# Keys' stage: ScalarE instead of VectorE normalises the rows of x

## The reference, cut to what matters

```python
xn = _layernorm(x, axis=-1)            # (x - m) / sqrt(v + 1e-5), for each row
x = x + gnn(xn, edge_index, ...) + linear_attention(xn[None], Wq, Wkv, Wproj, bproj)[0]
x = x + lstm_layer(_layernorm(x), ...)

# in linear_attention: keys are elu(k) + 1, and the context is a sum over all rows
k = jax.nn.elu(k) + 1.0
k_sum = k.sum(axis=2)
context = jnp.einsum('bhnd,bhne->bhde', k, v)
```

## Time and profile before

| | us |
|---|---|
| median of 3 runs | 2197.34 |
| lowest, highest | 2193.83, 2198.04 |
| the profiled execution | 2199.32 |
| its span | 2197.5 |
| DVE, ACT, PE busy in the span | 1598.0, 1186.0, 1941.3 |
| DVE, ACT, PE busy at 0 to 184 us | 146.48, 103.39, 125.95 |

### The profile page before, as it was taken

One profiled execution on the slowest core, in us unless ns is written; L12 is line 12 of the kernel. 1 busy time (PEld: TensorE's weight loads), 2 busy tenths in 40 slices (PEclk: granted clock), 3 DMA queues, 4 the chain that ended last, 5 costly groups with the idle time before them and its releaser, 6 DMA issues.

```text
span 2197.5 us, 42640 instructions
## 1 busy us (share of the span) xinstructions
PE 1941.3 (88%) x13254; PEld 1547.4 (70%) x13254; DVE 1598.0 (73%) x4208; ACT 1186.0 (54%) x3147; POOL 197.2 (9%) x274
## 2 busy tenths in 40 slices
PE   5679989999999999999989989996679998899845
PEld 4567876666666666666658878885468887888833
DVE  7887878777777777777737967777876666566687
ACT  4574445555555555555534446666875665566527
POOL 3352001000000000000002200000000000000060
PEclk8799998999999999999999999997569999899975
DMA  4222320100100100100115312223543343234403
GB/s 126 87 80 83 95 98 21 34 24 26 33 24 26 32 25 26 32 26 26 31 46 163 90 51 112 112 112 126 162 138 102 123 125 111 86 123 125 120 2 117
DMA packets 96796, 170.48 MB, mean 78 GB/s; under 512 B 8213, under 2 KB 68841, under 8 KB 96384
## 3 DMA queue, kind: packets, MB, share of 16 engines
q1 hardware_dynamic: 67693, 86.80, 12.2%
q10 hardware_dynamic: 27248, 77.11, 11.4%
q0 software_dynamic: 1744, 5.21, 0.8%
HBM read 110.53 MB, written 58.56 MB: 77 GB/s over the span
## 4 chain that ended last, share of the span: by engine, by line
PE 59%; DVE 21%; ACT 10%; issue 8%; POOL 2%; DMA 1%; DVEq 0%; ACTq 0%; POOLq 0%; SPq 0%
PE psum L665 28%; PE psum L814 11%; PE psum L660 7%; PE psum L771 4%; ACT scr L1121 2%; DVE scr L1503 2%; ACT scr L1129 2%; DVE scr L1713 2%; DVE bufB L1715 1%; DVE bufB L1630 1%; DVE scr L1711 1%; PE psum L848 1%; ACT scr L1088 1%; DVE bufA L1831 1%; PE psum L609 1%
## 5 line engine op out<-in xcount | busy, mean ns | idle before, releaser
L665 PE MATMUL psum<-halves,counts 128*128 128x512 f32 x2401 | 759.5, 423 | 16.3 <-ACT counts L1026 16.3
L1528 DVE TENSOR_TENSOR wx<-rs_buf 128x392 bf16<-128x392 bf16 (+1 forms) x1568 | 545.3, 391 | 211.4 <-PE psum L660 207.7
L1026 ACT ACTIVATE counts<-psum 128x392 fp32r<-128x392 f32 x784 | 391.4, 499 | 356.4 <-PE psum L660 355.0
L814 PE MATMUL psum<-bufB,wx 128*128 128x125 f32 x3392 | 425.3, 284 | 32.2 <-DVE bufB L1715 21.2
L814 PEld LDWEIGHTS psum<-bufB,wx 128*128 128x128 f32 x3392 | 401.3, 194 | 56.3 <-DVE bufB L1715 37.8
L665 PEld LDWEIGHTS psum<-halves,counts 128*128 128x128 f32 x2401 | 393.8, 190 | 65.9 <-ACT counts L1026 21.8
L660 PEld LDWEIGHTS psum<-wx 128*128 128x128 bf16 x3136 | 170.6, 99 | 198.5 <-issue 191.6
L660 PE MATMUL psum<-wx 128*128 128x98 bf16 x3136 | 284.7, 213 | 4.0 <-DVE wx L1528 2.9
L771 PE MATMUL psum<-bufA,wx 128*128 (+1 forms) x800 | 181.7, 379 | 3.2 <-POOL rs_buf L526 3.2
L771 PEld LDWEIGHTS psum<-bufA,wx 128*128 128x128 f32 x800 | 147.9, 190 | 20.7 <-issue 3.4
L1129 ACT ACTIVATE scr<-scr 128x125 f32<-128x125 f32 x280 | 86.4, 309 | 120.9 <-DVE scr L1713 115.6
(11 more groups left out here) (262 smaller groups left out, 2521.5 us busy)
## 6 DMA issues: line engine op xcount, KB each, us to landing
bufA<-gates_of_x ACTq DMA_DIRECT2D x136, 500.0 KB, 3.4
gates_of_x<-bufB SPq DMA_DIRECT2D x24, 1000.0 KB, 3.9
x_times_eps_plus_sums<-scr SPq DMA_DIRECT2D x50, 128.0 KB, 1.7
sums_by_feature<-scr SPq DMA_DIRECT2D x50, 128.0 KB, 1.9
scr<-x_times_eps_plus_sums SPq DMA_DIRECT2D x49, 128.0 KB, 2.1
wx<-in_x_dram SPq DMA_DIRECT2D x25, 250.0 KB
x_plus_mix<-wx SPq DMA_DIRECT2D x25, 250.0 KB, 4.8
bufB<-x_plus_mix SPq DMA_DIRECT2D x25, 250.0 KB, 2.7
```

What stands on the lines that cost most here:

```text
L665: return mm(psum[:, 3 + v, :], cnt[v][:, hi, :], xhl[:, hi, :, :].rearrange("p s d -> p (s d)"), start=(hi == 0), stop=(hi == NT - 1))
L814: return mm(gate_half(u, m, gate), whhv[:, k, (2 * gate + m) * P:(2 * gate + m + 1) * P], h, start=False, stop=(k == 1), skip_group_check= ...
L1026: fn(cnt[v][:, :, c * u:c * (u + 1)], psum[:, CB[u % 4], 0:PER * KEYS].rearrange("p (c h) -> p h c", h=NT), ACT.Copy).then_inc(S["c_sb"], 1)
L1528: last = tt(to, tab2[:, 0:k_, :].unsqueeze(1).broadcast_to([P, PER // 2, k_, 2]), keysT[v][:, part_, g0:g0 + PER // 2, :].unsqueeze(2).bro ...
```

## The change

ScalarE now normalises the rows: x * rstd + shift, as one activation (Identity) with a scale and a bias per row. VectorE computes the shift, -mean * rstd, for the whole chunk at once, behind the reciprocal (`row_scale`). ScalarE's new `row_norm` waits for it on its first tile of a chunk. The places in ScalarE's loop are the same as they were in VectorE's: after the scaled row of tile i-1, two tiles at i % 5 == 2, two at 3, one at 4. For the first chunk ScalarE does five normalisations right behind the square root, ahead of the copies L949. A buffer `shift` of 128x5 is added, twice.

```diff
@@ -175,6 +175,7 @@
         stats = sb("stats", XT * 6)
         mv = [sb(f"mv{v}", XT * 2) for v in range(2)]
         rstd = [sb(f"rstd{v}", XT) for v in range(2)]
+        shift = [sb(f"shift{v}", XT) for v in range(2)]
         eps_ln = sb("eps_ln", 1)
         tick = sb("tick", 32)
         ctxb = sb("ctxb", 2 * P)[:, :].rearrange("p (a n) -> p a n", a=2)
@@ -943,7 +944,16 @@
                 fn(rstd[q % 2][:, 0:h], mv[q % 2][:, :].rearrange("p (t c) -> p t c", c=2)[:, 0:h, 1], ACT.Sqrt,
                    bias=eps_ln[:, :]).then_inc(S["ln_std"], 1)
 
+            def row_norm(q, j):
+
+                if j == 0:
+                    act.wait_ge(S["ln_r"], 2 * q + 2)
+                fn(x_ring[q % XR][:, j, :], x_ring[q % XR][:, j, :], ACT.Identity, bias=shift[q % 2][:, j:j + 1],
+                   scale=rstd[q % 2][:, j:j + 1]).then_inc(S["xn_ok"], 1)
+
             row_std(0)
+            for j in range(XT):
+                row_norm(0, j)
             for n, (_, to) in enumerate(groups):
                 act.wait_ge(S["tr_ps"], n + 1)
                 fn(to, psum[:, 4 + n, :].rearrange("p (j n) -> p j n", j=4), ACT.Copy).then_inc(S["tr_sb"], 1)
@@ -983,6 +993,11 @@
                                       row_out[:, 2:j + 1, :]).then_inc(S["row_in2"], 16)
                 if i % XT == 1 and i // XT + 1 < XCH:
                     row_std(i // XT + 1)
+                q, j = i // XT + 1, i % XT
+                if j >= 2 and q < XCH:
+                    for j_ in ((0, 1), (2, 3), (4,))[j - 2]:
+                        if j_ < len(tiles(q)):
+                            row_norm(q, j_)
 
             act.wait_ge(S["lo_q"], NT)
             act.wait_ge(S["ld_small"], 128)
@@ -1287,14 +1302,14 @@
                         last = dve.bn_aggr(mv[q % 2][:, 2 * t:2 * t + 2], stats[:, 6 * t:6 * t + 6])
                     last.then_inc(S["ln_v"], 1)
 
-            def row_norm(q, j):
-
-                if j == 0:
-                    dve.wait_ge(S["ln_std"], q + 1)
-                    dve.reciprocal(rstd[q % 2][:, 0:len(tiles(q))], rstd[q % 2][:, 0:len(tiles(q))]).then_inc(S["ln_r"], 1)
-                    dve.wait_ge(S["ln_r"], q + 1)
-                ts(x_ring[q % XR][:, j, :], x_ring[q % XR][:, j, :], mv[q % 2][:, 2 * j:2 * j + 1],
-                   rstd[q % 2][:, j:j + 1], ALU.subtract, ALU.mult).then_inc(S["xn_ok"], 1)
+            def row_scale(q):
+
+                h = len(tiles(q))
+                dve.wait_ge(S["ln_std"], q + 1)
+                dve.reciprocal(rstd[q % 2][:, 0:h], rstd[q % 2][:, 0:h]).then_inc(S["ln_r"], 1)
+                dve.wait_ge(S["ln_r"], 2 * q + 1)
+                stt(shift[q % 2][:, 0:h], mv[q % 2][:, :].rearrange("p (t c) -> p t c", c=2)[:, 0:h, 0], -1.0,
+                    rstd[q % 2][:, 0:h], ALU.mult, ALU.mult).then_inc(S["ln_r"], 1)
 
             def row_cut(t):
 
@@ -1420,8 +1435,7 @@
 
             for j in range(XT):
                 row_stats(0, j)
-            for j in range(XT):
-                row_norm(0, j)
+            row_scale(0)
             dve.wait_ge(S["tr_sb"], 4)
             dve.memset(psum[:, 6, :], 0.0).then_inc(S["m_z"], 1)
             constants()
@@ -1445,10 +1459,8 @@
                         small_vectors()
                         for j_ in range(XT):
                             row_stats(1, j_)
-                    if j >= 2 and q < XCH:
-                        for j_ in ((0, 1), (2, 3), (4,))[j - 2]:
-                            if j_ < len(tiles(q)):
-                                row_norm(q, j_)
+                    if j == 2 and q < XCH:
+                        row_scale(q)
                     q, j = (t - 1) // XT + 2, (t - 1) % XT
                     if t and q < XCH and j < len(tiles(q)):
                         row_stats(q, j)
```

## The result

The change makes the kernel slower: 2206.66 us in the median of six runs (2202.66 to 2213.00), beside 2196.44 for the kernel before (2193.83 to 2198.32). The ratio is 1.0045, with an interval of 1.0034 to 1.0056: about +10 us, where 2196.0 was forecast and 2203.0 was the upper end of the range.

What follows compares the result with a forecast made beforehand. No engine was simply the bound: VectorE, ScalarE and TensorE form a ring in the keys' stage. Gains and losses by period sum to -1.35 us, on the median 2197.34 giving 2196.0 us; range 2190.5 to 2203.

Steps and rivals of the forecast that it cites:

- Added to VectorE: Ten shift instructions of 128x5 in the keys' stage, taken at 0.16 us each, bounds 0 and 0.21.
- A new wait: ScalarE's first normalisation of a period waits for VectorE's shift: start at 140.50, copy 1.61 us later, next minimum +1.10 us.
- T0: Reference time in a clean period: the minimum of the period's second tile, 139.12 us in the profile before.
- the second clean period: The period from 148.6 us, without other VectorE work on top: same steps, one mask wait of 0.21 less, -0.1 us.
- The tail: End of the keys' stage, from the minimum at 166.36: no statistics left to hide anything, +1.1 us.
- Opening: Before the first period: five normalisations delay ScalarE's weight copies 2 us, but VectorE stands 4.06 us for a DMA: 0.
- a ring that loses behind ScalarE's wait what VectorE wins: Keys' stage: at a period's first two normalisations the next minimum comes 1.10 us later, against 1.07 us VectorE had spent.
- ScalarE's normalisation: 49 Identity activations of 128x256 on ScalarE: 0.51 us each from start to start, bounds 0.40 and 0.60, 2.55 per period.
- Short masks: VectorE's masking after a late minimum takes 0.28 us, not 0.70, bringing the high part forward by 0.35 us.
- ScalarE becomes the bound: Rival: ScalarE's part grows 3.14 us a period, waits don't absorb it, TensorE's clock may stay low; +7.2, 2204.5 us; chance 0.13.
- The relief rival: VectorE was the bound and is relieved: 13.8 us won in six periods, less 1.4; 2184.9 us; chance 0.17.
- A wait for ln_r far from 0.6 us: Sign that the forecast is wrong: ScalarE's wait for VectorE's shift, put at 0.59 us a period, differs much.

Runs made afterwards that it cites:

- e8: Kernel before, with all five normalisations of a chunk moved on VectorE into its idle stretch ahead of the second tile's sum; 0.9948 times the kernel before.
- e9: Changed kernel with reciprocal and shift placed between VectorE's minimum and mask of the third tile, not behind the mask; 1.0005 times the kernel before.
- e11: The changed kernel timed again without any edit, on another chip; 1.0055 times the kernel before.
- e3: Changed kernel without the 49 normalisations, done by nobody; reciprocal and shift stay on VectorE; 0.9955 times the kernel before.
- e1: Changed kernel with reciprocal and shift moved ahead of the second tile's sum, where VectorE waits for the exponential; 1.0001 times the kernel before.
- e4: Kernel before plus 44 extra Identity activations on ScalarE into a spare buffer, waiting for nothing; VectorE normalises as before; 1.0011 times the kernel before.
- e12: Kernel before with all five normalisations in VectorE's idle stretch and 44 extra ScalarE activations into a spare buffer; 0.9994 times the kernel before.
- e2: Changed kernel with the shift's instruction issued twice, the first into a spare buffer; 1.0058 times the kernel before.

## Why the prediction was wrong

The failed step is "*Added to VectorE*", the shift at 0.16 us with bounds of 0 and 0.21, and with it "*A new wait*", by which ScalarE starts at 140.50. The shift takes 0.69 there, so ScalarE starts at T0 + 1.89 and not T0 + 1.38: 0.51 us later, and with everything queued behind it. It is a term of the right kind and the wrong size, and it explains about half of the miss. The bounds came from the reciprocal, the row of the same shape. The place should have given them. In the trace of before, GpSimd's low half starts ahead of the instruction behind the reciprocal, which starts at 140.29:

```profile
...
140.24 0.73 POOL L469 TENSOR_TENSOR halves<-wx,scr 128x256 fp32r<-128x256 f32 x1 [0.23 <-DVE scr L1306]
...
```

The pair of normalisations that stood there took 1.15, where e8's five take 1.70. The Trainium skill (VectorE: DVE Perf Modes, "Two Vector instructions with no wait between them") has a Vector instruction with two SBUF tensor inputs read the second through an interface shared with GpSimd. The shift, which reads `mv` and `rstd`, and the reciprocal, which reads one buffer, agree with it: 0.69 against 0.18 beside a running GpSimd instruction (the reciprocal's case is e9). Two inputs aren't all that matters in these rows, though: the mask has one, and takes 0.70 beside GpSimd's addition and 0.28 without it.

A check of its price in time: e11 and e9 differ by 8.5 us of earlier starts and by 10.8 us. On a straight line between them, an estimate that puts all of e9's gain down to the earlier starts, 0.51 us in nine stretches are worth 5.8 us, and at one for one 4.6, of the 11.6 between the forecast's -1.35 and +10.2.

How far it goes in single stretches: the second clean period ran at full clock throughout; forecast -0.1, and 0.51 more is +0.4; measured +0.46. The tail: 1.1 + 0.51 = 1.6; measured +1.75. Over nine stretches the term is 4.6 us, which would turn the forecast's -1.35 into +3.2. The stage end moved by 7.3 with the opening 1.07 earlier, so the nine stretches gave 8.4: 9.7 more than forecast, 4.6 of it by this term.

Some 2.7 us more stand in the first matmuls behind the late copies. At 29.6, 53.2, 128.9 and 145.4 us they took 2.08, 2.07, 2.07 and 1.52, against 1.69 and three times 1.13 before. They are longer because TensorE went wholly or partly at its lower clock; why it did there stays open. Nor was the clock lower throughout: from 22.6 us on the first stretch had 0.69 before and 0.76 after, that from 67.6 us 0.68 and 0.76. The remaining 2.4 us lie mainly in three stretches, by the table less these two terms: 0.9 in the one from 135.2, 0.7 in that from 22.6 and 0.4 in that from 42.8; no single row answers for them. This splitting of the last five us is read from the profiles, not tested, and the two us by which the medians moved more are not in it: here the profile of before, on which the forecast was built, is itself slow. Its wait of 4.06 us, against 1.9 to 3.2 in five kernels with the same opening, is what made "*Opening*" a 0.

Point by point:
- The mechanism, a ring that loses behind ScalarE's wait what VectorE wins, had the right parts. e3, e1 and the change stand at -10, 0 and +10: the relief, ScalarE's work, and the wait. Its balance was wrong: the first pair loses 1.96 us (the next minimum at T0 + 4.86 for + 2.90) and not 1.10, against 1.07 won. Of the 0.86 more, about 0.5 are the shift and 0.39 the matmul at 1.52.
- ScalarE's normalisation: 0.51 from start to start was right (143.95 to 144.95 for two is 0.50). The shift "done at 140.47" is 140.45 by its own terms, which changes nothing. No table load was added.
- Short masks came as forecast: 284 ns in the median after, 704 before. What they gave was less than the wait took.
- VectorE and ScalarE at 40 to 60 us: forecast near 18 and near 11, measured 16.99 and 11.11.
- The rival "*ScalarE becomes the bound*" had the right sign and named 2204.5, and its own sign came true: the clean stretch from T0 to the next table load, 9.49 before, is 11.65 after, over the 10.4. Its conditions hardly did: activations of 0.59 us, and at 40 to 60 us a clock of 0.83 against 0.84. ScalarE's work costs little while VectorE is late (e4), but 10 us once VectorE is relieved (e12), which is the change's case; that part of the rival was right, and the relief of e3 pays for it (e1). What turned the sum to a loss is a dear wait. "A wait for ln_r far from 0.6 us" was named as what would show the forecast wrong. Counted as there, from 0.46 us after the scaled row, it is 1.10.
- The relief rival: relief alone is worth 10 us (e3), near its 12.4, but ScalarE's share takes all of it back even without the dear wait (e1).

Whether the forecast's own wait of 0.59 us would have given 2196 isn't measured, and the runs speak against it. e9, with ScalarE 0.44 us earlier than in the forecast, stands at +0.5 (1.0005, 0.9996 to 1.0014), and the straight line from there to e11 passes the forecast's start at about +5.5. So about half of the miss lies outside the shift's term. The profiles point at the longer matmuls and the opening; no run tests it, and the cause of that half stays open.

## What to carry to other kernels

When work moves to another engine, price the small instruction that the new wait hangs on by its place, not by its shape: what GpSimd does at that moment, and what is queued in order behind the waiting engine. In a ring of engines moving work gives little either way (e1); first look for a stretch where the engine that has the work stands idle for another's table load, and put the work there (e8, -0.5%). A load that costs 2.4 us while another engine is late (e4) costs some 10 once that engine has been relieved (e12). And a difference of half a per cent should not be worked out on a single profile: this one held a wait of 4.06 us that was 1.9 to 3.2 us in five other kernels with the same opening.

## What was not expected of the hardware

A scalar_tensor_tensor of 128x5 with both inputs in SBUF takes 166 ns with no GpSimd computation beside it. When a GpSimd tensor_tensor is running it ends 0.01 to 0.03 us after that one does, however much is left: 0.69 when GpSimd's 0.72 us have just begun (the change, nine of nine), 0.36 when about half are left (e9), 0.18 when they are nearly over (e1 at 131.68). The one right behind it takes 153 ns (e2). A reciprocal of the same size takes 0.18 either way (e9). Five normalisations in a row run 0.32 us apart in e8, almost all of it with no GpSimd instruction beside them, where a pair in the old place held VectorE for 1.07.
